# A gated cross-attention block with a quantised feed-forward: projection, maximum, rounding and turning redone

## What is computed

```
a = LN(x) @ Wq + bq;  k, v = ctx @ Wk + bk, ctx @ Wv + bv        # 16 heads of 16
attn = softmax over the 16 heads of  q.k / 4                     # axis 0: heads, not keys
x = x + tanh(g_xattn) * (attn @ v @ Wo + bo)
s = sigmoid(clip_x) * max|LN(x)| / 127;  xq = clip(round(LN(x) / s), -128, 127) * s
gate, up = xq @ quant(w_gate).T, xq @ quant(w_up).T              # 704 columns
h = silu(gate) * up;  hq = the same fake quantisation of h, with max|h| over everything
x = x + tanh(g_ffn) * (hq @ quant(w_down).T)
```

## Time and profile before

| | us |
|---|---|
| median of three runs | 935.7 (935.19, 935.70, 940.88) |
| the profiled execution's own time | 934.85 |
| its span, first to last instruction | 933.1 |
| busy: PE / DVE / ACT / POOL | 763.3 / 812.1 / 721.2 / 500.9 |
| mean granted PE clock | 0.96 of full speed |

### The profile page before, as it was taken

One profiled execution on the slowest core, in us unless ns is written; L12 is line 12 of the kernel. 1 busy time (PEld: TensorE's weight loads), 2 busy tenths in 40 slices (PEclk: granted clock), 3 DMA queues, 4 the chain that ended last, 5 costly groups with the idle time before them and its releaser, 6 DMA issues. The chain is left out here.

```text
span 933.1 us, 20554 instructions
## 1 busy us (share of the span) xinstructions
PE 763.3 (82%) x8047; PEld 426.7 (46%) x8056; DVE 812.1 (87%) x1034; ACT 721.2 (77%) x1085; POOL 500.9 (54%) x342
## 2 busy tenths in 40 slices
PE   4998787777777579989999999999999885277476
PEld 2564351122121245656566666666566574133133
DVE  3899439999999779998999999999999969778678
ACT  3454449999999788888999998999999414499583
POOL 0334551000000019998999999999989954144300
PEclk9999899999999899999999999999999998599879
DMA  9696886565655376797677857696666661000013
GB/s 285 232 313 209 260 214 136 140 173 151 161 114 215 94 217 197 227 338 241 168 199 224 296 171 196 169 319 201 175 186 168 240 191 36 0 1 1 0 60 121
DMA packets 97933, 164.19 MB, mean 176 GB/s; under 512 B 9584, under 2 KB 36848, under 8 KB 97520
## 3 DMA queue, kind: packets, MB, share of 16 engines
q1 hardware_dynamic: 97840, 162.90, 58.8%
HBM read 133.50 MB, written 41.94 MB: 188 GB/s over the span
## 5 line engine op out<-in xcount | busy, mean ns | idle before, releaser
L929 POOL TENSOR_TENSOR e<-e,recip 128x768 f32<-128x768 f32 (+3 forms) x256 | 387.5, 1555 | 220.0 <-DVE recip L971 220.0
L898 ACT ACTIVATE e<-ps_att 128x512 f32<-128x512 f32 x512 | 301.2, 646 | 37.2 <-PE ps_att L839 36.5
L960 DVE TENSOR_REDUCE pair_sums<-e 128x128 f32<-128x2048 f32 x128 | 292.6, 2286 | 25.5 <-ACT e L898 25.4
L839 PE MATMUL ps_att<-arena 128*128 128x128 bf16 x2048 | 193.8, 220 | 3.8 <-ACT ps_att L906 3.8
L854 PE MATMUL acc<-e,arena 128*32 128x128 f32 x4096 | 178.9, 292 | 6.8 <-DVE e L941 3.6
L839 PEld LDWEIGHTS ps_att<-arena 128*128 128x128 bf16 x2048 | 150.3, 98 | 63.5 <-ACT e L898 4.2
L678 ACT ACTIVATE copies<-ps_max 128x1024 bf16<-128x1024 f32 x189 | 175.6, 1087 | 0.0
L835 PE MATMUL ps_att<-shift,minus 128*128 128x512 bf16 x384 | 149.7, 390 | 17.0 <-DMA arena<-k_stack 10.4
L854 PEld LDWEIGHTS acc<-e,arena 128*32 128x32 f32 x4096 | 105.0, 110 | 37.7 <-POOL e L929 9.0
L693 DVE TENSOR_TENSOR high<-copies,high 128x3072 bf16<-128x3072 bf16 x63 | 111.1, 1763 | 0.4 <-ACT copies L678 0.4
L941 DVE TENSOR_TENSOR e<-e,recip_v 128x256 f32<-128x256 f32 (+3 forms) x256 | 93.9, 414 | 0.0
(11 more groups left out here) (138 smaller groups left out, 860.9 us busy)
## 6 DMA issues: line engine op xcount, KB each, us to landing
arena<-k_stack SPq DMA_DIRECT2D x256, 256.0 KB, 3.1
arena<-q_stack SPq DMA_DIRECT2D x64, 256.0 KB, 4.9
k_stack<-parts SPq DMA_DIRECT2D x40, 256.0 KB, 3.8
q_stack<-parts SPq DMA_DIRECT2D x40, 256.0 KB, 3.7
k_stack<-k_stack SPq DMA_DIRECT2D x12, 512.0 KB, 11.2
arena<-in_x_dram SPq DMA_DIRECT2D x5, 1024.0 KB, 8.1
arena<-in_ctx_dram SPq DMA_DIRECT2D x4, 1024.0 KB, 6.6
arena<-q_stack SPq DMA_DIRECT2D x8, 512.0 KB, 8.2
```

What stands on the lines that cost most here:

```text
L839: last = nc.tensor.matmul(bank[:, j * P:(j + 1) * P], ks[:, i % KRING, b * P:(b + 1) * P], qs[:, h, b * P:(b + 1) * P], start=False, stop= ...
L898: nc.scalar.activation(e_at(qc * STEPS + i, half * HB, (half + 1) * HB).rearrange("p q b i -> p b q i"), ps[(qc * (2 * STEPS) + 2 * i + ha ...
L929: nc.gpsimd.tensor_tensor(part, part, by_pairs(recip[:, kc % 2, :], share), ALU.mult).then_inc(pool_scaled, 1)
L960: nc.vector.tensor_reduce(pair_sums[:, :, h // 2, :], e[:, g % RING // 2].rearrange("p q s b i -> p q i (s b)"), AX.X, ALU.add).then_inc(s ...
```

## The change

- The fp32 bias `bo` becomes three bf16 rows whose sum it is (`bo_parts`, 32 equal partitions each). It is loaded and split at the start of `attend`. PE adds it with a matmul of `ones_w` (1/32) ahead of the four products of a pair. `psY` has five slots.
- ACT scales the pair out of PSUM into `xn`, POOL adds x, DVE goes on with the statistics. `ve`, `tmp` and `newton` lie in PSUM.
- ACT's order per chunk: four scaled pairs of chunk c, then eight normalisations of chunk c-1.
- Tokens are turned in fp32 by PE, straight from `xn` (block 0 already in the projection block), ACT multiplies by the scale and converts out of PSUM into 16-bit integers, and DVE clips these into `xqT`. `psX` has one buffer per half.
- The gate tiles are all 128 wide (`wT` padded with zeros, cleared in `attend`), and the clearing of `hs` goes.
- The second maximum over partitions: PE turns the column to a row, DVE reduces it, PE spreads it.
- Down: ACT converts into 16-bit integers in two halves, DVE clips once.

```
# attend
+   sp.dma_start(out_s[:, 0:D], bcast_rows(bo, D)).then_inc(bo_loaded, 16)       # SP, ahead of all
+   def split_bias():                                                           # POOL, ahead of all
+       step = Chain(pool, bo_split)
+       left, parts = out_s[:, 0:D], keep["bo_parts"]
+       mid, low = slice(32, 64), slice(64, 96)
+       pool.wait_ge(bo_loaded, 16)
+       step(nc.gpsimd.tensor_copy(parts[:], left[0:96]))
+       nc.gpsimd.tensor_tensor(left[mid], left[mid], parts[mid], ALU.subtract)
...
+       step(pool.memset(keep["wT"][:, :, :, I:IC * P], 0.0))
# projection
+   def turn(pe, n):
+       for m in range(DC):
+           if n:
+               pe.wait_ge(s["rounded"], DC * (n - 1) + m + 1)
+           for k in range(TB):
+               last = nc.tensor.transpose(psX[:, m, k * P:(k + 1) * P], xn[:, n * TB + k, m * P:(m + 1) * P],
+                                          ident_f[:])
+           last.then_inc(s["xn_turned"], 1)
# PE, per pair n
+   if n >= SLOTS: pe.wait_ge(s["y_scaled"], n - SLOTS + 1)
+   nc.tensor.matmul(psY[:, n % SLOTS, :], ones_w[:], bo_parts[:]....to_broadcast([PARTS * 32, 2, D]), ...)
...
+   turn(pe, 0)                                   # behind the last pair
# ACT
+   nc.scalar.activation(xn[:, 2 * n:2 * n + 2, :], psY[:, n % SLOTS, :]..., ACT.Copy, scale=tanh_g[:, 0:1])
+   for c in range(NC):
+       for b2 in range(PAIRS):
+           scaled(c * PAIRS + b2)
+           if c and b2 == 1: root_of(c - 1)
+       if c:
+           normal(2 * c - 2)
+           if c == NC - 1: root_of(c)
+           normal(2 * c - 1)
+   normal(NB - 2)
# POOL, per pair n
+   nc.gpsimd.tensor_tensor(x2[:, t, :], xn[:, t, :], x2[:, t, :] if c else keep["x_first"][:, t, :], ALU.add)
# DVE
-   residual(c * PAIRS + b2)
-   if b2: statistics(c * PAIRS + b2 - 1)
+   statistics(c * PAIRS + b2)
# gate and up, ACT
+   def rounds(n):
+       if n >= 2: act.wait_ge(s["xqT_ready"], n - 1)
+       for m in range(DC):
+           act.wait_ge(s["xn_turned"], DC * n + m + 1)
+           nc.scalar.activation(xi[:, n % 2, m], psX[:, m], ACT.Copy, scale=x_scale[:, 2:3]).then_inc(s["rounded"], 1)
-   if j == 1 and n + 3 < NB: rounds(n + 3)
-   if j == 3 and n + 1 < NB: turned(n + 1)
+   if j == 2 and n + 1 < NB: rounds(n + 1)
# DVE
+   nc.vector.tensor_scalar(xqT[:, n % 2], xi[:, n % 2], -QMAX - 1.0, QMAX, ALU.max, ALU.min).then_inc(s["xqT_ready"], 1)
-   if j == 0 and n + 2 < NB: integers(n + 2)
+   if j == 4 and n + 1 < NB: integers(n + 1)       # behind the product of tile 4
# PE
+   if j == 1 and n + 1 < NB: turn(pe, n + 1)
...
+   nc.tensor.matmul(turned_max[0:1, 0:P], amax[:, 2:3], ident_f[:], ...).then_inc(s["hmax_turned"], 1)
+   pe.wait_ge(s["top_ready"], 1)
+   nc.tensor.matmul(spread_max[:, 0:1], ones_row[:], top[:], ...).then_inc(s["hmax_all"], 1)
# down, ACT
-   nc.scalar.activation(hs[:, n], hs[:, n], ACT.Copy, scale=h_scale[:, 2:3], bias=MAGIC)
-   nc.scalar.activation(hq[:, n % 2, DVE_H:IC], hs[:, n, DVE_H:IC], ACT.Copy, bias=-MAGIC)
+   for j in (0, IC // 2):
+       nc.scalar.activation(hi[:, n % 2, j:j + IC // 2], hs[:, n, j:j + IC // 2], ACT.Copy, scale=h_scale[:, 2:3])
# DVE
+   if n == 0: clipped(0, 0, IC // 2)
...
+   clipped(n, 0 if n else IC // 2, IC).then_inc(s["hq_ready"], 1)
```

More of the change, by code:

```diff
@@ L16 @@
 BF16 = mybir.dt.bfloat16
+I16 = mybir.dt.int16
 ALU = mybir.AluOpType
@@ L92 @@
 KRING = 4
+PARTS = 3
 NT = NC * B
@@ L912, in chunk @@
                                 act.wait_ge(stored, 16 * B * (qc - 1))
+                            else:
+                                act.wait_ge(bo_split, BO_STEPS)
                             gather(qc * STEPS)
@@ L1048, in _ @@
                 def _(pool):
[L1050 to L1059, removed]
+                    pool.memset(ones_w[:], 1.0 / 32).then_inc(s["ones_set"], 1)
+                    add_identity(pool, ident_f[:], 1.0, s["id_f"])
+                    for n in range(NT // 2):
+                        c = n // PAIRS
+                        t = slice(2 * n, 2 * n + 2)
+                        if n % PAIRS == 0:
+                            pool.wait_ge(x_loaded[c], 16)
+                        pool.wait_ge(s["y_scaled"], n + 1)
+                        nc.gpsimd.tensor_tensor(x2[:, t, :], xn[:, t, :], x2[:, t, :] if c else keep["x_first"][:, t, :],
+                                                ALU.add).then_inc(s["x2_ready"], 1)
                     pool.wait_ge(s["xmax_ready"], 1)
@@ L1085, in _, with scaled @@
                     act.wait_ge(s["tanh_ready"], 1)
+                    def scaled(n):
+                        act.wait_ge(s["y_ready"], n + 1)
+                        nc.scalar.activation(xn[:, 2 * n:2 * n + 2, :],
+                                             psY[:, n % SLOTS, :].rearrange("p (a d) -> p a d", a=2), ACT.Copy,
+                                             scale=tanh_g[:, 0:1]).then_inc(s["y_scaled"], 1)
                     def root_of(c):
@@ L1225, in rounds @@
                     def rounds(n):
[L1226 to L1230 removed]
                         if n >= 2:
[L1232 to L1238 removed]
+                            act.wait_ge(s["xqT_ready"], n - 1)
+                        for m in range(DC):
+                            act.wait_ge(s["xn_turned"], DC * n + m + 1)
+                            nc.scalar.activation(xi[:, n % 2, m], psX[:, m], ACT.Copy, scale=x_scale[:, 2:3]
+                                                 ).then_inc(s["rounded"], 1)
+                    rounds(0)
                     for n in range(NB):
@@ L1251, in _ @@
                                     act.wait_ge(s["h_pool"], m - 1)
-                                nc.scalar.activation(up[0:rows, m % 2, :], psU[0:rows, k % UB, :], ACT.Copy,
-                                                     scale=gscale[0:rows, IC + j:IC + j + 1]).then_inc(s["u_ready"], 1)
-                            if j == 1 and n + 3 < NB:
-                                rounds(n + 3)
-                            if j == 3 and n + 1 < NB:
-                                turned(n + 1)
+                                nc.scalar.activation(up[:, m % 2, :], psU[:, k % UB, :], ACT.Copy,
+                                                     scale=gscale[:, IC + j:IC + j + 1]).then_inc(s["u_ready"], 1)
+                            if j == 2 and n + 1 < NB:
+                                rounds(n + 1)
                 @block.vector
@@ L1339, in _ @@
                             if j == 1 and n + 1 < NB:
-                                turn(n + 1)
-                            rows = rows_of(j)
+                                turn(pe, n + 1)
                             k = n * IC + j
```

202 lines of the change are left out of this document (90 added, 112 removed).

## The result

The changed kernel takes 929.6 us (median of 20 runs, 924.8 to 937.6), the kernel before 937.4 in the same comparison (934.0 to 948.1). The ratio is 0.992, with a 95% interval of 0.991 to 0.994: 7 us less by the ratio, 7.8 by the medians, where 10.4 were forecast. The stages are compared by windows in the profiled executions, 931.07 us after and 934.85 before. The rows answer to those of the earlier trace rows; the columns are window, length, busy PE, PE weight load, DVE, ACT and POOL (with counts), granted clock, DMA share, GB/s.

The account below looks back on a forecast made before the run. No engine was full, so each stage was read by its chain (ACT bounding gate, DVE down). Terms 3.7+4.9-8.5+3.4+1.5+5.4 gave 10.4 less than 934.85: 924.4, with 0.85 added 925.3, called 925; own range 919 to 931, stated range 916 to 935.

Parts of the forecast that it names:

- the main case: Whole kernel: the late clip ties gate blocks together while the other stages gain; 925 us, chance 0.50.
- Gate and up: Gate stage: PE starts each block behind DVE's late clip and ACT idles twice; 70.2 against 61.7 us, plus 8.5.
- six times 8.86: Gate stage, blocks 1 to 6: a period of 8.86 us each, which was four times 8.05 and twice 7.1.
- Projection: Projection: PE adds the bias, POOL adds x, ACT's order sets shifts 9.3 us apart; minus 3.7 us.
- Rival E: Projection: three engines in a row and ACT's lock lengthen each cycle by 1.2, no gain; 929 us, chance 0.15.
- Restart: Last token maximum to first gate matmul: two ACT conversions, a clip, PE's start, 2.2 for 7.1 us; minus 4.9.
- Maximum: Second maximum: two small fp32 matmuls and a DVE reduction take 1.5 us in place of 4.87; minus 3.4.
- Down: Down stage: PE starts 3.6 us after the block begins, not 5.17 (minus 1.5); blocks take 3.5 us, not 4.53 (minus 5.4).
- its bound of 4: Down stage: the total comes 4 us below the forecast if PE's clock is already up there.
- B: Gate stage: the late clip costs nothing since ACT holds enough tiles; period 6.56 + 1.05, 917.5 us, chance 0.13.
- C: Gate stage: DVE's clip stands still while POOL works, up to 1.2 us in seven blocks; 933.5 us, chance 0.12.
- D: Gate and down stages: DVE clips int16 at one element per cycle, 3.36 us for 3072 columns; 944 us, chance 0.10.

Follow-up runs that it names:

- experiment 4: Changed kernel with PE making the four matmuls of the last tile twice in blocks 0 to 6: 924.8 us, ratio 0.986 to the kernel before.
- experiment 5: Changed kernel with PE doing eight fp32 transposes, or four bf16 matmuls, while waiting for the clip: 923.5 us (transposes) and 926.6 us (matmuls).
- Experiment 6: Changed kernel with the second maximum over partitions on POOL again, as before: 930.8 us, ratio 0.995 to the kernel before.
- experiment 1: Changed kernel with DVE's clip of the next block ahead of its product of tile 4, not behind: 914.65 us, ratio 0.977 to the kernel before.
- experiment 3: Changed kernel with both moves, the clip ahead of the product of tile 4 and transposes ahead of tile 3: 912.7 us, ratio 0.973 to the kernel before.
- the repeat: The kernel of experiment 3 unchanged, timed again beside the reordered projection: 909.7 us, ratio 0.971 to the kernel before.
- experiment 8: Kernel of experiment 3, with ACT scaling two next-chunk pairs between its normalisation groups and DVE's second maximum one step later: 907.3 us, ratio 0.968 to before.
- experiment 7: Changed kernel with the down stage's old rounding (ACT rounds and converts a third, DVE converts two thirds and clips): 938.0 us, ratio 1.000 to before.
- experiment 2: Changed kernel with PE turning the next block ahead of tile 3, not tile 1, clip still late: 919.8 us, ratio 0.982 to the kernel before.

## Why the prediction was right and wrong

**Where it stands.** 925 was forecast, 929.6 measured: the sum was -10.4, the medians say -7.8. The mechanism of the main case was right in each stage; one term was mis-sized, by 5.1 us in the profile. That the total came as near is in part luck: the clock's early rise in the down stage gave 2.5 back.

**Gate and up, +8.5 forecast, +13.6 measured.** The late clip, PE's start behind it, the two gaps of ACT and the period stood as worked out (8.72 against 8.86, PE's start 1.22 against 1.32, the gaps 1.01 and 1.05 against 1.25 and 1.05). The term failed in the step "six times 8.86": it held PE at full clock through the stage. In four blocks PE fell to 1.2 GHz for 3.4 us, and 1.68 each makes 6.7. The prediction did reckon with PE's clock at the first block and in the down stage, but took it as full in between without a reason. PE's idle time would not have warned it: 2.1 us in a block of 8.72 stand against 1.9 in before's 8.04. Experiments 4 and 5 separate the period from the clock: more work on PE, same period, no fall. Less the fall, +6.9 remain, some 1.5 under the forecast: the six periods were 0.14 shorter each (0.8), and block 0 lasted 9.6 from PE's start, not 10.2.

**Projection, -3.7 forecast, -2.7 measured.** The shifts' spacing was right (9.3). The profile of after began at part clock, which moved the first shift by 1.6. In kernels with the same code the stage took 44.95 to 47.86, a gain of 1.5 to 4.4 against the 49.32 of before. Where PE was at full clock from the start, as in before, it took 44.95 or 44.96 in all three, and the first shift came 15.8 behind attention, as forecast: like with like the change gives 4.4. Rival E (no gain) is refuted.

**Restart, -4.9 and -4.9.** Two conversions, 1.26, and the clip, 0.43, as priced. Most of the 0.46 of PE's start was the missing record, in the row of before as in this profile; in the other ten the matmul starts some 0.05 behind the clip. In the gate stage the two 512-column conversions take 1.27 from start to end, and ACT's next silu starts 1.14 behind the start of the first, against 1.18 in the sum.

**Maximum, -3.4 forecast, -3.15 measured.** 1.72 in place of 1.5: each fp32 matmul is recorded as two, 0.58 in all, at half clock, where the estimate took less.

**Down, -1.5 and -5.4 forecast, -1.5 and -7.9 measured.** The start was exact, and the steady block is PE's 3.5 as forecast. The surplus is chance of the clock: it rose 3.5 us behind the first `psD` in this profile, 9.4 before; in the other kernels with the new rounding 3.3 to 9.6, and the stage took 29.4 to 32.0. The latest rise is that of experiment 5 with transposes:

```profile
879.82 32.00 PE L1450 MATMUL psD<-wd_T,hq 128*128 128x256 bf16 x192 [5.21 <-DVE hq L1403]
```

Its 32.0, with a rise at 9.6, against the 37.4 of before, with one at 9.4, are the 5.4 that were forecast. The forecast had kept the late rise (11.0 for two blocks) and named the other as its bound of 4. Experiment 6 took away the small matmuls and the clock still rose early (4.9).

**The rivals.** B is refuted by experiment 1. C, the clip held by POOL: all seven clips take 0.41 or 0.42, but they met POOL's product for 0.07 us only. In experiment 3 the clip made during block 0 starts together with a product of POOL. The clip takes 0.42 there, and it is the product that is longer, 1.55 where the others take 1.27:

```profile
814.76 1.55 POOL L1349 TENSOR_TENSOR arena<-up,sil 128x512 f32<-128x512 f32 x1 [1.23 <-ACT up L1290]
```

In the repeat it is 0.42 and 1.45, and in experiment 8 a clip that starts within a product takes 0.54. The Trainium skill (GPSIMD Engine Reference, "Key points") speaks of SBUF interfaces shared with DVE; these few meetings agree in kind, and cost 0.1 to 0.3 us, not the 1.2 of rival C. D, the slow int16: 0.42 for 1024 and 0.95 for 3072 columns are the prices of bf16. The Trainium skill (VectorE: DVE Perf Modes, "What auto-detection actually checks") had it so, and the trace agrees.

**What stays open.** What brings the clock down is known only by cases, one profile of each kernel: it fell in three or four blocks of each of the three kernels that have some 24 matmuls and eight fp32 transposes in a period of 8.7 us and nothing to fill the wait (the changed kernel, experiments 6 and 7), each of the ten times within 0.4 us of PE's start behind the wait of 1.24. It never fell where either gap of PE was gone: the 1.24 (experiments 1, 4 and 5), the 0.70 (experiment 2, in 7.85) or both (experiment 3), nor in the kernel before, with bf16 transposes, 0.72 and 1.16 in 8.04. One rival is left: the kernels with the wait filled ran on one chip and experiments 6 and 7 on another. The kernel before took 937.1 us on both beside experiments 1 to 4 and 6 to 8, and the period with both moves was 6.80 on both, so nothing speaks for the chip, but no kernel whose clock fell was run beside a filled one. Nor do the runs say why it falls in some blocks of a kernel and not in their like, why it rises sooner or later in the down stage, or why attention's end varies by 7 us.

## What to carry to other kernels

Where the order of the programs is written by hand, an operation moved behind another engine's late result ties two blocks together: for each instruction that releases the next block ask what stands ahead of it in its own engine's program; here the clip needed nothing of the product, and stood behind it. Put work that only prepares the next block where the bounding engine has tiles in store, not where it has run dry: the same eight transposes ahead of tile 3 and not tile 1 shortened the period by 0.9 us. And read PE's granted clock block by block, as a term of its own: its falls cost here as much as the whole change gained, though PE idled hardly longer in a block than before.

## What the hardware showed that I had not expected

- More work on PE made the gate stage shorter: with 28 matmuls or 56 transposes that nobody needs, no block took the 10.4 us of four blocks of the changed kernel, all inner ones took 8.72, and PE's granted clock stayed at 1.00.
- fp32 transposes of 128x128 served for that as well as bf16 matmuls of 512 columns.
- POOL's `partition_all_reduce` is 0.38 us long and yet starts 4.4 after its input is there: 5.95 us of "issue" lie between POOL's last product and it. The same instruction at the first maximum, where POOL had been idle for 9.92, starts 0.14 behind its input, which suggests, untested here, that the price depends on what POOL did just before. Two tiny matmuls and a DVE reduction of one row take 1.72, even at half clock.
- ACT converts fp32 out of PSUM into int16 at the price of a copy (0.68 for 512 columns, as for the scaled copies), and DVE clips int16 into bf16 as it does bf16: rounding costs no pass of its own.
- The clock rose between 3.3 and 9.6 us after PE began in the down stage of kernels with the same code there, and in the first 3 us of the projection it was 0.66 in one profile and 1.00 in others: the stage's time moved by up to 3 us with it, as much as some of the terms that one wants to measure.
